# Edge-network pass of a four-layer graph kernel: target rows held as two float32r halves in place of three bf16 parts

## The chip, the cores and the metric

The kernel runs on one core of one Trainium2 chip. The metric is device time in microseconds (us) of one execution; lower is better. The median of three runs of the kernel before is 6998.53 us.

## The reference

A graph of 6250 nodes (128 features each) and 106250 edges, sorted by target, passes through four layers, each added to x after a layer norm and a relu: layer 0 (messages of neighbours and relations), layer 1 (mixture of experts, three rounds of gathering), layer 2 (the edge network), layer 3 (three dense rounds). The change is about layer 2 and the table that is made for it at the end of layer 1:

```python
def _L2_gnn_ref(x, src, dst, W1, b1, W2, b2, W4, b4):
    theta = x[dst] - x[src]
    w = sigmoid(relu(theta @ W1 + b1) @ W2 + b2)
    agg = segment_sum(w * theta, dst)
    indeg = segment_sum(ones, dst)
    return agg + indeg * (x @ W4 + b4)
```

Since (x[dst] - x[src]) @ W1 + b1 = (x @ W1 + b1)[dst] - (x @ W1)[src], the kernel makes y = x @ W1 once for each node. For each edge it then needs the row of the target, y + b1, and the row of the source, y and x.

## The kernel before

**Tiling.** Edges go in tiles of 128 (P). Four tiles (GROUP) are a group, 16 tiles (RING) a turn; there are 832 tiles, 208 groups and 52 turns. The targets of a group lie in a window of 64 nodes (WIN), since edges are sorted by target.

**Tables.** `parts_yb` holds y + b1 for each node as three bf16 parts (PARTS = 3, 384 bf16 values), whose sum is the float32 value. `rows_yh` holds y and h in float32. Both are written in the last round of layer 1 by `Layer1Out`: `late_dve` (line 1758) makes the row y + b1 in `u` and cuts it with `cut_dve` (lines 898 to 903: cut, remainder, cut, remainder), and `late_sp` (line 1724) stores `cut` and `yh`. There are 49 blocks of nodes.

**The pass** (`edge_pass` with `edge_net`, lines 442 to 790). The engines work side by side and are ordered by semaphores alone; each engine runs its own list in order.

- GpSimd (line 563) gathers the source rows of a tile, 128 rows of 1 KB, by an indirect DMA into one of 16 slots of `ring`. It waits until `tiles_done` says that the tile 16 back is finished.
- ScalarE (lines 569 to 615) issues the load of `ywin`, the 64 target rows of a group, two groups ahead (`load_window`, line 584), and of `relb`, the targets' places (line 576). It copies the finished sums of a group out of PSUM (`copy_sums`, line 591) and takes the sigmoid (line 603).
- VectorE makes the one-hot matrices: `onehot_t`, 64 x 1024 for 8 tiles (line 637), and `onehot` (line 639). `dots` (lines 646 to 654) makes the hidden layer and its product with W2 for a group; line 664 weights the one-hot by the sigmoid (`onehot_w`); lines 693 and 695 add the sums of a group to `acc`.
- TensorE brings the target rows to the edges (`hidden_net`, line 715): for each tile, three products `onehot_t` x part into `zt`, 64 x 128 weights and 128 columns (line 725). Line 756 sums the weighted source rows by target (`by_target`, one float32 product for each tile, 129 columns). `turn_sums` (lines 735 and 736) turns the sums of a group.

**Order on TensorE for a group n** (`net_tile`, line 739): the products of `zt` for tiles 0, 1 and 2 of group n+1, `turn_sums(n-1)`, `zt` for tile 3 of group n+1, then a wait for `onehot_w` of group n and the four products of `by_target`, which raise `tiles_done`. Between them lie the products of `Layer2` for a block of nodes (lines 1852 to 1862), spread over 16 tiles or so by `over` (line 488). The load of `ywin` is awaited before tile 0 of a group.

Of the kernel before, what the change touches and what calls it, by code (L numbers as in the profile page):

```python
# [7 lines left out]
D = 128  # L8
H = 256
# [3 lines left out]
P = 128  # L13

GROUP = 4
WIN = 64
RING = 16
HALF = RING // 2
GROUPS = RING // GROUP
# [14 lines left out]
NPAD = NB * P  # L34
# [28 lines left out]
FP = mybir.dt.float32  # L63
F16 = mybir.dt.float16
B16 = mybir.dt.bfloat16
PARTS = 3
LAST_GROUP = TURNS * GROUPS - 1
YH = 2 * D
FR = mybir.dt.float32r
I32 = mybir.dt.int32  # L70
U32 = mybir.dt.uint32
ALU = mybir.AluOpType
# [82 lines left out]
def gnn_kernel(nc, t, out):  # L155
    ctx = ExitStack()
    with ctx:
# [3 lines left out]
        def dram(name, shape, dt=FP):  # L161
            return nc.dram_tensor(name, shape, dt, kind="Internal").ap()
# [8 lines left out]
        def sbuf(name, shape, dt=FP):  # L171

            uses[0] += 1
            return nc.sbuf_tensor(f"{name}_{uses[0]}", shape, dt)
# [8 lines left out]
        rows256 = [dram(f"rows256_{k}", [NPAD, H]) for k in range(2)]  # L183

        parts128 = [dram(f"parts128_{k}", [NPAD, PARTS * D], B16) for k in range(2)]
        parts256 = [dram(f"parts256_{k}", [NPAD, PARTS * H], B16) for k in range(2)]
        rows_yh = dram("rows_yh", [NPAD, YH])
        parts_yb = dram("parts_yb", [NPAD, PARTS * D], B16)
        x_first = dram("x_first", [NPAD, D])
        x_rows = dram("x_rows", [NPAD, D])  # L190
        rdeg_dram = dram("rdeg_dram", [NPAD])
# [250 lines left out]
        def edge_pass(table, width, work, edge_net=None, prologue=None):  # L442
# [11 lines left out]
            with ExitStack() as tmp:  # L454
# [10 lines left out]
                    names += ["fold_pe", "fold_act", "fold_dve", "fold_own"]  # L465
                if edge_net:
                    (w2, b2) = edge_net
                    onehot_t = tmp.enter_context(sbuf("onehot_t", [WIN, 2, HALF * P], B16))
                    relb = tmp.enter_context(sbuf("relb", [WIN, 2, HALF * P]))
                    ywin = tmp.enter_context(sbuf("ywin", [WIN, GROUPS, PARTS * D], B16))  # L470
                    hidden = tmp.enter_context(sbuf("hidden", [P, GROUP, D]))
                    dot = tmp.enter_context(sbuf("dot", [P, 2, GROUP]))
                    weight = tmp.enter_context(sbuf("weight", [P, 2, GROUP]))
                    onehot_w = tmp.enter_context(sbuf("onehot_w", [P, 2, GROUP, WIN]))
                    zt = tmp.enter_context(psum("zt", [P, 2, GROUP, P]))
                    by_target = tmp.enter_context(psum("by_target", [WIN, 2, 512]))
                    held_sums = tmp.enter_context(sbuf("held_sums", [WIN, 2, D + 1]))
                    names += ["rel_loaded0", "rel_loaded1", "z_done", "net_own", "dot_done", "weight_done",
                              "weighted", "copied", "turned"] + [f"ywin_loaded{g}" for g in range(GROUPS)]

                def programs(block, sems, loop):

                    sem = dict(zip(names, sems))
# [85 lines left out]
                    def _(act):  # L569
# [10 lines left out]
                        def load_window(i, g):  # L580
                            w = act.value_load(win[0:1, bass.ds(i * GROUPS + g, 1)], min_val=0, max_val=SPARE)

                            act.wait_ge(tiles_done, i * RING + GROUP * (g + 1))
                            act.dma_start(ywin[:, g, :], parts_yb[bass.ds(w, WIN), :]).then_inc(sem[f"ywin_loaded{g}"], 16)

                        def copy_sums(n):

# [122 lines left out]
                    def _(pe):  # L710
# [4 lines left out]
                        def hidden_net(i, k):  # L715

                            g, q = divmod(k, GROUP)
                            if k % HALF == 0:
                                pe.wait_ge(onehot_ready, i * 2 + (k // HALF + 1))

                            pe.wait_ge(gathered[k], i * 16 + 16)
                            if q == 0:
                                pe.wait_ge(sem[f"ywin_loaded{g}"], i * 16 + 16)
                            for c in range(PARTS):
                                last = nc.tensor.matmul(zt[:, g % 2, q, :], onehot_t[:, g // 2, (k % HALF) * P:(k % HALF + 1) * P],  # L725
                                                        ywin[:, g, c * D:(c + 1) * D], start=(c == 0), stop=(c == PARTS - 1))
                            if q == GROUP - 1:
                                last.then_inc(sem["z_done"], 1)

# [197 lines left out]
        def rows_of(table, b, lo=0, hi=None):  # L927
            return table[bass.ds(b * P, P), lo:(hi or table.shape[1])]
# [91 lines left out]
        class Layer1(Work):  # L1020
# [12 lines left out]
            ACT_LATE = ""  # L1033
            DVE_LATE = "mix6 next_row" + Work.CUT

# [508 lines left out]
        class Layer1Out(Layer1):  # L1544
# [7 lines left out]
            DVE = Layer1.ROUTE + "mix0 mix1 mix2 mix3 down_b0 down_b1 down_b2 down_b3 mix4 mix5 with_row"  # L1552
            PE_LATE = "down2 down3 h2_t h2_w"
            ACT_LATE = "norm_root h_row h2_t_sb"
            DVE_LATE = "mix6 mix7 new_x " + Work.NORM_DVE + " next_y y_b1" + Work.CUT + " next_h"

            def __init__(self, cur, w, last):
                super().__init__(cur, None, w)
# [2 lines left out]
            def buffers(self, tmp):  # L1561
                s, p = super().buffers(tmp)
                s |= {n: tmp.enter_context(sbuf(n, sh)) for n, sh in
                      (("rt", [P, 2, P]), ("x", [P, D]), ("st", [P, 12]), ("hn", [P, D]), ("hnt", [P, P]), ("u", [P, D]),
                       ("part", [P, D]), ("yh", [P, YH]))}
                return s, p

            def fold_banks(self, n):
# [155 lines left out]
            def late_sp(self, sp, m, i, b):  # L1724
                s, _ = self.b
                sp.wait_ge(self.sem["block_out"], i * 48 + 16)
                sp.nop(nofuse=True)
                sp.dma_start(s["x"][:, :], rows_of(x_rows, b)).then_inc(self.sem["late_in"], 16)
                yield 4
                m.need(self.dve2, "new_x")  # L1730
                self.stored(m, [(rows_of(x_rows, b), s["x"][:, :])])
                m.need(self.dve2, "next_h")
                self.stored(m, [(rows_of(parts_yb, b), s["cut"][:, 0:PARTS * D]), (rows_of(rows_yh, b), s["yh"][:, :])])
                if not self.in_pass:
                    sp.wait_ge(self.sem["block_out"], i * 48 + 64)
                    sp.nop(nofuse=True)
                yield RING
# [20 lines left out]
            def late_dve(self, dve, m, i, b):  # L1758
                s, p = self.b
# [21 lines left out]
                dve.wait_ge(self.sem["block_out"], i * 48 + 16)  # L1781
                m.done("next_y", nc.vector.tensor_copy(s["yh"][:, 0:D], p["misc"][:, 0:D]))
                m.done("y_b1", nc.vector.tensor_tensor(s["u"][:, :], p["misc"][:, 0:D], self.last["b1"], ALU.add), wait=True)
                self.cut_dve(m, s["u"][:, :], s["left"][:, 0:D], [s["cut"][:, c * D:(c + 1) * D] for c in range(PARTS)])
                m.done("next_h", nc.vector.tensor_copy(s["yh"][:, D:H], s["hn"][:, :]))

        class Layer2(Work):
# [76 lines left out]
        def edge_codes(block_base, column_of, places, begin, wn, wl, embp):  # L1864
# [10 lines left out]
            with ExitStack() as tmp:  # L1875
# [19 lines left out]
                with phase(nc, bank, "own_s", "consts", "shifted", "masked", "compared", "counted", "coded", "spilled",  # L1895
# [87 lines left out]
                    def _(sp):  # L1983
# [4 lines left out]
                        sp.wait_ge(zeroed, 1)  # L1988
                        sp.dma_start(emb[0:RELS - whole, REL_BLOCKS - 1, :], t["L0_gnn_rel_emb"][whole:RELS, :]).then_inc(loaded, 16)
                        spare = []  # L1990
                        for table, width in ((rows256[0], H), (rows256[1], H), (rows_yh, YH)):
                            spare += [table[SPARE:NPAD, c:c + P] for c in range(0, width, P)]
                        for dst in spare:
                            sp.dma_start(dst, zeros[:, :]).then_inc(stored, 16)
                        spare16 = []
                        for table, width in ((parts256[0], PARTS * H), (parts256[1], PARTS * H), (parts_yb, PARTS * D)):
                            spare16 += [table[SPARE:NPAD, c:c + P] for c in range(0, width, P)]
                        for dst in spare16:
                            sp.dma_start(dst, zeros[:, 0:P // 2].bitcast(B16)).then_inc(stored, 16)
# [1252 lines left out]
        with ExitStack() as lay:  # L3252
            w = expert_tables(lay)
# [49 lines left out]
```

## Time and profile before

| | us |
|---|---|
| median of three runs | 6998.53 (6994.68 to 7003.74) |
| profiled execution, from its first to its last instruction | 7889.6 |
| of it, the passes of layer 1 that gather (2250 to 5190) | 2940 |
| of it, the edge-network pass (5190 to 6520) | 1330 |
| of it, the dense rounds of layer 3 (6600 to 7890) | 1290 |

The profiled execution is the only one with a trace. It is 891 us longer than the median of the runs, and the trace does not say which stages that time belongs to. PE is TensorE, PEld its weight loads, DVE VectorE, ACT ScalarE, POOL GpSimd, SP SyncE. The granted clock is given as a share of 2.4 GHz: 0.50 is the lower level, 1.2 GHz. Busy times of PE are unions of pipelined instructions, each of which is longer than the distance to the next one. A float32 product shows as two weight loads and two matmuls, a bf16 product as one of each.

### The profile page before, as it was taken

To read this page: it belongs to the slowest core of one execution; us is meant where nothing else is said; L and a number is where in the kernel's file an instruction comes from. 1 tells how busy PE (TensorE), PEld (TensorE's weight loads), DVE (VectorE), ACT (ScalarE), POOL (GpSimd) and SP (SyncE) were. 2 spreads that over 40 slices of the span, in tenths; PEclk is the share of its full clock that TensorE was granted. 3 is DMA by queue.
4 is the path that set the end of the run, shared out by engine and by line. 5 is a ranking of instruction groups with operands and counts; after the bars stand their busy time and mean duration, and the time that the engine had idled before them with its cause. 6 is when DMAs were issued, how large, how long until landed. Compare 5 with 4: busy or idle time off the path is not lost. (4 is left out here: it accounts for less than half of the span.)

```text
span 7889.6 us, 137900 instructions
## 1 busy us (share of the span) xinstructions
PE 6633.2 (84%) x47136; PEld 4683.6 (59%) x47136; DVE 3780.3 (48%) x11316; ACT 2080.9 (26%) x6122; POOL 2537.4 (32%) x2577
## 2 busy tenths in 40 slices
PE   4999789999978888887777877867777777999999
PEld 2555446666657777776666666645555554555555
DVE  7787534444444444443444444456666662222111
ACT  3555312222222222222333333322222220000000
POOL 0000000000035555554555555546666660000000
PEclk6999989999989999998999998955555558999999
DMA  5343442222245445444455454434444446555654
GB/s 160 107 136 113 131 131 88 89 88 86 78 124 148 144 143 145 141 141 138 138 144 145 142 144 138 138 89 126 127 125 126 126 124 201 196 193 196 200 192 160
DMA packets 669788, 1085.73 MB, mean 138 GB/s; under 512 B 247170, under 2 KB 495206, under 8 KB 667043
## 3 DMA queue, kind: packets, MB, share of 16 engines
q1 hardware_dynamic: 474722, 508.53, 21.1%
q0 software_dynamic: 147584, 438.73, 19.7%
q10 hardware_dynamic: 46784, 129.65, 4.6%
q8 instruction: 379, 6.21, 0.3%
q14 instruction: 319, 2.61, 0.1%
HBM read 902.64 MB, written 174.06 MB: 136 GB/s over the span
## 5 line engine op out<-in xcount | busy, mean ns | idle before, releaser
L563 POOL DMA_INDIRECT ring<-parts,src_idx x1664 | 1626.4, 977 | 1314.1 <-issue 444.7
L2695 PE MATMUL agg_ps<-sheet,big 128*128 128x448 f16 x6090 | 1182.0, 354 | 23.6 <-DMA sheet<-adj 23.6
L563 POOL DMA_INDIRECT ring<-rows_yh,src_idx x832 | 840.0, 1010 | 540.7 <-issue 226.0
L1099 ACT ACTIVATE strong<-hid,s_b 128x128 f32<-128x128 f32 x2352 | 668.3, 369 | 1160.9 <-PE hid L1208 441.1
L2695 PEld LDWEIGHTS agg_ps<-sheet,big 128*128 128x128 bf16 x6090 | 598.2, 99 | 565.8 <-DMA sheet<-adj 25.9
L1208 PE MATMUL hid<-agg,big 128*128 128x128 f32 x6272 | 806.3, 281 | 62.2 <-issue 51.6
L1208 PEld LDWEIGHTS hid<-agg,big 128*128 128x128 f32 x6272 | 774.9, 197 | 136.0 <-issue 119.1
L1196 PE MATMUL y<-big,strong 128*128 128x256 f32 x3136 | 742.8, 385 | 13.7 <-issue 12.0
L683 DVE TENSOR_TENSOR acc<-acc,sums 128x128 f32 x416 | 120.3, 289 | 1120.8 <-DMA acc<-in_edge_type 759.5
L1196 PEld LDWEIGHTS y<-big,strong 128*128 128x128 f32 x3136 | 586.4, 191 | 98.4 <-issue 18.5
L713 PE MATMUL sums<-onehot,ring 128*128 128x64 bf16 x9984 | 412.0, 196 | 174.8 <-issue 134.8
L1233 PE MATMUL hid<-big,agg 128*128 128x512 f32 x784 | 513.1, 788 | 35.7 <-DVE agg L1115 33.4
L713 PEld LDWEIGHTS sums<-onehot,ring 128*128 128x128 bf16 x9984 | 378.5, 100 | 272.7 <-issue 254.6
L756 PE MATMUL by_target<-ring,onehot_w 128*64 128x129 f32 x1664 | 408.8, 427 | 139.0 <-DVE onehot_w L664 109.0
L1110 DVE SCALAR_TENSOR_TENSOR row<-y,gate,row 128x256 f32<-128x256 f32 x392 | 191.1, 487 | 531.7 <-PE y L1196 433.5
L756 PEld LDWEIGHTS by_target<-ring,onehot_w 128*64 128x64 f32 x1664 | 328.4, 223 | 184.5 <-issue 184.5
L2359 PE MATMUL counts_ps<-hot_col,hot 128*128 128x392 bf16 (+3 forms) x1960 | 349.8, 300 | 90.4 <-DVE hot_col L2226 86.4
L3032 POOL MEMSET acc<- 128x6400 f32 x1 | 5.4, 5432 | 1164.5 <-PE counted_ps L3066 1164.5
L725 PE MATMUL zt<-ywin,onehot_t 64*128 64x128 bf16 x2496 | 344.4, 306 | 16.2 <-DMA ring<-rows_yh,src_idx 12.8
L1087 ACT ACTIVATE weak<-weak 128x512 f32<-128x512 f32 x294 | 184.8, 628 | 643.7 <-DVE weak L1139 571.3
L2914 DVE SCALAR_TENSOR_TENSOR agg<-agg_ps,counts_hold,acc 128x448 f32<-128x448 f32 x42 | 28.7, 684 | 674.3 <-PE agg_ps L2695 674.3
L2226 DVE TENSOR_SCALAR hot_col<-column_of,held 128x539 bf16<-128x539 f16 (+2 forms) x1176 | 337.4, 344 | 0.0
(443 smaller groups left out, 9757.7 us busy)
## 6 DMA issues: line engine op xcount, KB each, us to landing
sheet<-adj SPq DMA_DIRECT2D x294, 784.0 KB, 4.1
sheets<-adj SPq DMA_DIRECT2D x74, 784.0 KB, 4.2
adj<-big ACTq DMA_DIRECT2D x7, 5488.0 KB
adj<-acc ACTq DMA_DIRECT2D x7, 5488.0 KB
relb<-rel_rows ACTq DMA_DIRECT2D x106, 256.0 KB
ring<-parts,src_idx POOLq DMA_INDIRECT x1664
big<-adj SPq DMA_DIRECT2D x24, 784.0 KB, 4.7
parts<-cut SPq DMA_DIRECT2D x98, 192.0 KB, 1.9
```

The costliest lines, as they stand in the source:

```text
L563: nc.gpsimd.indirect_dma_start(ring[:, k, 0:YH] if edge_net else ring[:, k, :], None, table, bass.IndirectOffsetOnAxis(ap=src_idx[:, i * R ...
L713: return nc.tensor.matmul(ap, lhs, rhs, start=first, stop=last, skip_group_check=True)
L725: last = nc.tensor.matmul(zt[:, g % 2, q, :], onehot_t[:, g // 2, (k % HALF) * P:(k % HALF + 1) * P], ywin[:, g, c * D:(c + 1) * D], start ...
L756: last = nc.tensor.matmul(by_target[:, g % 2, 0:D + 1], onehot_w[:, g % 2, j, :], ring[:, g * GROUP + j, D:YH + 1], start=(j == 0), stop=( ...
L1099: ins = nc.scalar.activation(s["strong"][:, e % 2, j, :], p["hid"][:, bank_at, j * P:(j + 1) * P], ACT.Relu, bias=self.w["s1_b"][:, e, j:j ...
L1110: m.done(name, nc.vector.scalar_tensor_tensor(out=out, in0=expert, scalar=self.b[0]["gate"][:, e:e + 1], in1=so_far, op0=ALU.mult, op1=ALU ...
L1196: ins = nc.tensor.matmul(y, s["strong"][:, e % 2, k, :], w["s2"][:, k, e, :], start=(k == 0), stop=(k == 3))
L1208: ins = nc.tensor.matmul(p["hid"][:, bank_at, j * P:(j + 1) * P], w["s1"][:, k, e, j * P:(j + 1) * P], s["agg"][:, k, :], start=(k == 0), ...
L1233: ins = nc.tensor.matmul(hid, s["agg"][:, k, :], w["weak"][:, k, 2 * q:2 * q + 2, :].rearrange("p e f -> p (e f)"), start=(k == 0), stop=( ...
L2226: last = nc.vector.tensor_scalar(hot_col[:, w % 2, cut_at[j]:cut_at[j + 1]], column_of[:, lo * NODE_BLOCKS:hi * NODE_BLOCKS], held[:, r, n ...
L2359: return nc.tensor.matmul(ap, lhs, rhs, start=first, stop=last, skip_group_check=True)
L2695: ins = nc.tensor.matmul(ps[:, 0:HALF_COLS], rows_in[:, k * per + s, c, :], sheet[:, k, s * HALF_COLS:(s + 1) * HALF_COLS], start=(k == fi ...
```

## The change

The table `parts_yb` becomes `halves_yb`, two float32 values for each feature; the first is the value written as float32r, the second what is left. In the edge pass `ywin` and `onehot_t` are float32r, and each tile takes two products where it took three. `Layer1Out` makes the halves with one copy and one subtraction instead of four operations.

```diff
-        parts_yb = dram("parts_yb", [NPAD, PARTS * D], B16)
+        halves_yb = dram("halves_yb", [NPAD, 2 * D])
...
-                    onehot_t = tmp.enter_context(sbuf("onehot_t", [WIN, 2, HALF * P], B16))
+                    onehot_t = tmp.enter_context(sbuf("onehot_t", [WIN, 2, HALF * P], FR))
-                    ywin = tmp.enter_context(sbuf("ywin", [WIN, GROUPS, PARTS * D], B16))
+                    ywin = tmp.enter_context(sbuf("ywin", [WIN, GROUPS, 2 * D], FR))
...
-                            act.dma_start(ywin[:, g, :], parts_yb[bass.ds(w, WIN), :]).then_inc(sem[f"ywin_loaded{g}"], 16)
+                            act.dma_start(ywin[:, g, :].bitcast(FP), halves_yb[bass.ds(w, WIN), :]).then_inc(sem[f"ywin_loaded{g}"], 16)
...
-                            for c in range(PARTS):
+                            for c in range(2):
                                 last = nc.tensor.matmul(zt[:, g % 2, q, :], onehot_t[:, g // 2, (k % HALF) * P:(k % HALF + 1) * P],
-                                                        ywin[:, g, c * D:(c + 1) * D], start=(c == 0), stop=(c == PARTS - 1))
+                                                        ywin[:, g, c * D:(c + 1) * D], start=(c == 0), stop=(c == 1))
...
+                s["y2"] = tmp.enter_context(sbuf("y2", [P, 2 * D], FR))
...
-                self.stored(m, [(rows_of(parts_yb, b), s["cut"][:, 0:PARTS * D]), (rows_of(rows_yh, b), s["yh"][:, :])])
+                self.stored(m, [(rows_of(halves_yb, b), s["y2"][:, :].bitcast(FP)), (rows_of(rows_yh, b), s["yh"][:, :])])
...
-                self.cut_dve(m, s["u"][:, :], s["left"][:, 0:D], [s["cut"][:, c * D:(c + 1) * D] for c in range(PARTS)])
+                m.done("high", nc.vector.tensor_copy(s["y2"][:, 0:D], s["u"][:, :]), wait=True)
+                m.done("low", nc.vector.tensor_tensor(s["y2"][:, D:2 * D], s["u"][:, :], s["y2"][:, 0:D].bitcast(FP),
+                                                      ALU.subtract))
```

The zeroing of the spare rows at the start takes two float32 stores for the new table where it took three bf16 stores.

## Rows read from the trace of the kernel before

**Rows 1.** Three stages by windows: busy time, instructions, granted clock, DMA share.
```profile
core 0: us, PE busy (x) PEld busy (x) DVE busy (x) ACT busy (x) POOL busy (x), PEclk, DMA share, GB/s
2250.00:5190.00 2940.00, 2382.15 (x22109) 1968.55 (x22109) 1340.98 (x4367) 847.77 (x2460) 1626.35 (x1664) 0.90 0.49 142
5190.00:6520.00 1330.00, 930.59 (x5072) 676.94 (x5072) 866.44 (x2177) 314.55 (x800) 840.01 (x832) 0.50 0.44 125
6600.00:7890.00 1290.00, 1266.03 (x7115) 714.38 (x7112) 242.05 (x756) 108.93 (x415) 20.97 (x36) 0.99 0.58 193
```

**Rows 2.** The gathers on POOL: durations, first and last start; two single ones.
```profile
L563 POOL DMA_INDIRECT ring<-rows_yh,src_idx x832: 940/946/1454, 5194.9 to 6499.8; - x167
...
5607.81 0.94 POOL L563 DMA_INDIRECT ring<-rows_yh,src_idx  x1 [0.30 <-issue]
5609.06 0.95 POOL L563 DMA_INDIRECT ring<-rows_yh,src_idx  x1 [0.30 <-issue]
```

**Rows 3.** Waits of 5190 to 6525: who, for whom, us in total, times, longest.
```profile
DVE hidden L646 <- DMA sheets<-adj: 288.7, 62, 7.2
POOL ring L563 <- issue: 226.0, 715, 1.9
PE sums L735 <- ACT held_sums L591: 178.5, 85, 7.0
POOL ring L563 <- DMA acc<-in_edge_type: 147.8, 62, 3.0
PE by_target L756 <- DVE onehot_w L664: 109.0, 77, 3.4
```

**Rows 4.** Timeline of TensorE in the edge pass, then one gather: start, length, instruction, count.
```profile
5604.20 1.14 PE L725 MATMUL zt<-ywin,onehot_t 64*128 64x128 bf16 x9
5605.13 0.31 PE L735 MATMUL sums<-ident,held_sums 64*128 64x64 f32 x1
5605.68 0.50 PE L725 MATMUL zt<-ywin,onehot_t 64*128 64x128 bf16 x3
5606.11 1.98 PE L756 MATMUL by_target<-ring,onehot_w 128*64 128x129 f32 x8
5608.02 0.80 PE L1862 MATMUL pa<-w,ht 128*128 128x128 f32 x2
...
5612.42 0.94 POOL L563 DMA_INDIRECT ring<-rows_yh,src_idx  x1 [2.42 <-DMA acc<-in_edge_type]
```

**Rows 5.** Lengths of single PE records by line: min/median/max in ns.
```profile
L725 PE MATMUL zt<-ywin,onehot_t x2496: 216/311/311, 5200.0 to 6511.2; 64*128 64x128 bf16 x192
...
L756 PE MATMUL by_target<-ring,onehot_w x1664: 422/422/476, 5207.8 to 6517.4; 128*64 128x129 f32 x185
...
L1857 PE MATMUL pb<-ones,wsum x98: 347/358/368, 5255.5 to 6526.6; 1*128 1x1 f32 x98
...
L2759 PE MATMUL xt_ps<-ident,acc x147: 272/273/303, 6591.5 to 7865.8; 128*128 128x128 f32 x147
```

**Rows 6.** Four-byte neighbours on PE: a run of transposes at full clock, and one-column products.
```profile
6625.67 0.60 PE L2759 MATMUL xt_ps<-ident,acc 128*128 128x128 f32 x4
...
5255.45 0.58 PE L1857 MATMUL pb<-ones,wsum 1*128 1x1 f32 x2
```

**Rows 7.** VectorE groups by form: the one-hot, and the nearest writes of four bytes.
```profile
L637 DVE TENSOR_SCALAR onehot_t<-relb,iota_col 64x1024 bf16<-64x1024 f32 x105 | 78.9, 751 | 7.9 <-DMA relb<-rel_rows 7.8
L2903 DVE TENSOR_SCALAR acc<-big 128x512 f32<-128x512 f32 x14 | 6.0, 427 | 0.5
L1925 DVE TENSOR_SCALAR int<-acc 128x1024 int32<-128x1024 int32 x2 | 2.2, 1104 | 0.0
```

**Rows 8.** The cut in the last pass of layer 1 (4050 to 5190), VectorE by form.
```profile
L901 DVE TENSOR_TENSOR left<-u,cut 128x128 f32<-128x128 f32 x40 | 11.7, 293 | 1.4
L900 DVE CAST cut<-u 128x128 bf16<-128x128 f32 x40 | 10.2, 254 | 1.4
L902 DVE CAST cut<-left 128x128 bf16<-128x128 f32 x40 | 9.1, 226 | 1.4
```

**Rows 9.** DMA of 5190 to 6520: a queue's packets, MB and share; one issue.
```profile
q10 hardware_dynamic: 25280, 38.13, 9.9%
...
ywin<-parts_yb ACTq DMA_DIRECT2D x210, 48.0 KB
```

More of the change, by code:

```diff
@@ L1554, in gnn_kernel @@
             ACT_LATE = "norm_root h_row h2_t_sb"
-            DVE_LATE = "mix6 mix7 new_x " + Work.NORM_DVE + " next_y y_b1" + Work.CUT + " next_h"
+            DVE_LATE = "mix6 mix7 new_x " + Work.NORM_DVE + " next_y y_b1 high low next_h"
             def __init__(self, cur, w, last):
@@ L1990, in _ @@
                         spare = []
-                        for table, width in ((rows256[0], H), (rows256[1], H), (rows_yh, YH)):
+                        for table, width in ((rows256[0], H), (rows256[1], H), (rows_yh, YH), (halves_yb, 2 * D)):
                             spare += [table[SPARE:NPAD, c:c + P] for c in range(0, width, P)]
@@ L1995, in _ @@
                         spare16 = []
-                        for table, width in ((parts256[0], PARTS * H), (parts256[1], PARTS * H), (parts_yb, PARTS * D)):
+                        for table, width in ((parts256[0], PARTS * H), (parts256[1], PARTS * H)):
                             spare16 += [table[SPARE:NPAD, c:c + P] for c in range(0, width, P)]
```

## The prediction

> **What bounds the kernel now.** I read the stages by windows first. The change touches one of them, the edge-network pass, 1330 of 7889.6 us, and a few operations of the pass before it [rows 1]. In the edge pass no engine is full: PE is busy 930.6 us (70%), DVE 866.4, POOL 840.0, and the clock of TensorE is at its lower level, 0.50, throughout; the layer-1 passes, where PE is busy 81%, have 0.90, the dense rounds at 98% have 0.99 [rows 1]. Then the gathers: one takes 0.946 us and 0.30 of issue before it, so 1.25 us, and 832 of them 1040 us; the first starts at 5194.9 and the last at 6499.8, 1305 us apart [rows 2]. That is 6.27 us for a group of four where POOL alone would need 5.0. The other 265 us are gathers that wait for a free slot, and slots come free when `by_target` on PE is done: the wait of 2.42 us in the timeline is one of them, and the waits list holds 62 like it, 147.8 us, named after a DMA that has nothing to do with it [rows 3, 4]. So the pass is a loop: gather, `zt` on PE, `dots` on DVE, sigmoid on ACT, `onehot_w` on DVE, `by_target` on PE, slot free, gather. PE's share of it, for one group, is 930.6 / 208 = 4.47 us; POOL's floor under it is 5.0 us.
>
> The profiled execution is 891 us longer than the median of the runs. VectorE's 288.7 us of waits before `hidden`, under the name of a DMA that doesn't belong there, come while PE's own records run on without a gap [rows 3, 4]; if such waits are smaller in the runs, the pass there is nearer to POOL's floor: scaled by 6998.5 / 7889.6 it would be 1180 us. I work out differences on the profiled execution and carry them over in us, and say where the floor would cut them.
>
> **The change part by part.** *The products of `zt`.* Before: nine matmuls in 1.14 us, the last 0.31 long, so (1.14 - 0.31) / 8 = 0.104 us each at clock 0.50, and three of them 0.312 us for a tile [rows 4, 5]. After: two float32r products. The trace has none. Bounds: as cheap as bf16, 0.104; or as dear as a float32 product, which is two records: eight records of `by_target` in 1.98 us are (1.98 - 0.42) / 7 = 0.22 each, 0.44 for a product [rows 4, 5]. Between them lies what I take for nearest: an operation that shows as a single record with operands of four bytes and 128 columns. That is the float32 transpose, four in 0.60 us at the full clock: (0.60 - 0.27) / 3 = 0.11, which is 0.22 at clock 0.50 [rows 1, 5, 6]. A second row points the same way: two records with 128 columns of float32 weights and one column of data take 0.58 us, so the second comes 0.58 - 0.36 = 0.22 us after the first although there is nothing to stream, and it is the load of four-byte weights that paces them [rows 5, 6]. I take 0.21 for a float32r product, two for a tile: 0.42, which is 0.11 us more than the three bf16 products. Over 832 tiles: +92 us of PE time. With the ends: 2 x 0.104 - 0.312 = -0.104, -87 us; and 2 x 0.44 - 0.312 = +0.57, +473 us.
>
> How much of +92 reaches the end: tiles 0 to 2 of a group stand before `turn_sums`, and that waits for ACT's copy in 85 of 208 groups [rows 3]; there their +0.33 us is hidden. In the other 123 groups it shows, 41 us. Tile 3 stands right ahead of `by_target`: 208 x 0.11 = 23 us. Where `by_target` waits for `onehot_w` anyway, in 77 groups [rows 3], it is hidden too: (41 + 23) x 131 / 208 = 40 us. POOL gives nothing back, since its waits for slots end with `by_target`; but in a run near its floor part of it would be covered. I take +40, between 0 and +92.
>
> *VectorE's one-hot.* `onehot_t` takes 0.751 us for 1024 columns and will write four bytes instead of two [rows 7]. A scalar compare with four bytes in and out takes 0.427 us for 512 columns, so it can stay at 0.75 to 0.8; the dearest row of that kind and size is 1.104 us, +0.35 x 105 = +37 us of DVE time, on an engine busy 65% [rows 1, 7]. A faster one is excluded by no row, but the present rate is already half the dearest. I take nothing, up to +15 of the 37 on the loop.
>
> *The load of `ywin`.* 64 rows of 1024 bytes, not 768. It is issued two groups ahead, some 12 us; its queue is 9.9% busy [rows 9]. It would cost only if it landed after tile 0 is due. Nothing. No instruction is added on ACT, and nothing queues behind it.
>
> *Layer1Out.* Two operations fewer for each of 49 blocks (0.226 and 0.293 us and some 0.035 each): 49 x 0.59 = 29 us of DVE time in a pass where DVE is busy 46% [rows 1, 8]. They are late work, awaited by SP's store alone, whose rows grow from 768 to 1024 bytes. Between 0 and -5 us; I take 0. The zeroing at the start is one small store less, 0.
>
> **The rivals.** *One pass at the bf16 rate (faster).* If a float32r product costs 0.104 us, PE loses 87 us of work. By the same shares (0.31 us in 123 groups, 0.104 in 208, times 131 / 208) 38 us reach the loop, 87 at most. For it: a float32 record of `by_target` takes 0.22 us for 129 columns, some 264 cycles of 1.2 GHz, two a column, as if the parts of a value went in one after the other; a type that sends one part would take one [rows 4, 5]. Against it: the single-record transpose and the paced weight loads [rows 6]. Time 6998.5 - 38 = 6960. The Trainium skill, "FP8 and Floating Point Precision", TensorE Precision Notes, says that the array works natively at about 22 bits, that a reduced-precision float32 operand is read as four bytes and truncated to that, and that true float32 takes four passes; by it this rival would hold. Against the change speaks "TensorE: Matmul & The Clock Gate", Weight-path perf modes: the fast weight load is for types other than float32. The trace has no float32r row to settle it.
>
> *Four passes, or the rate of float32 at this width (slower, much).* Each product 0.44 us: PE's work grows from 930.6 to 1404 us and PE becomes the bound of the pass. For it: every float32 product of the trace pays twice two cycles a column, at 129 columns as at 128 [rows 4]. Against it: it needs two records for each product, and the transposes show that four-byte operands can go in one [rows 6]. The pass would take 1404 us if PE has no gap: 1404 - 1330 = +74 in the profile, +224 against a pass of 1180, and +473 if all is added. I take +300: 7300. It decides as soon as PE needs more than POOL's 5.0 us for a group, that is from 4.47 + 0.53 us a group, or 0.22 us for a float32r product, on.
>
> *The clock rises (faster).* The pass has 0.50 at a PE share of 70%, its neighbour 0.90 at 81% [rows 1]. If the new products make PE denser (+92 or +473 us), the full clock might be granted. Every PE record would go at about twice the rate, 2.4 GHz for 1.2, the loop would shorten, and the 265 us of POOL's waits would largely go: some -150, 6850. Against it: a share of (930.6 + 92) / 1370 = 75% is nearer to the old value, and the gaps between the groups stay.
>
> **How the numbers follow.** Chances: the forecast (a product of 0.13 to 0.25 us) 0.39; one pass at the bf16 rate 0.25; float32's rate 0.26; the clock rises 0.10. The predicted time is the forecast's: 6998.5 + 40 = 7039, and its own range is 6990 to 7105 (0 to +92, and the +15 of VectorE). The range over all cases goes from 6950 (most of the bf16 case) to 7420 (most of the float32 case). Some 0.2% (14 us) is what a measurement of this kernel can tell from no change. Faster by more: 0.17 of the bf16 case's 0.25 and 0.09 of the clock's 0.10, 0.26. Within: 0.07 + 0.10 of the forecast + 0.01 = 0.18. Slower: 0.29 + 0.26 + 0.01 = 0.56.
>
> **What would show it.** In the profile after, the group of L725 has 1664 records if a float32r product is one record, 3328 if it is two. Six matmuls of `zt` in a row (tiles 0 to 2) give the price of one by their length: 0.83 us at 0.104, 1.4 at 0.21, over 2.4 at float32's rate. PE's busy time in the pass would be some 845, 1020 or 1400 us. The granted clock of the pass should stay 0.50, POOL's first and last gather should be about 1345 us apart, and L637 should stay under 0.8 us. The prediction is wrong if the clock of the pass rises, if `zt` is at bf16's rate and POOL's waits shrink with it, or if another stage (layer 1, layer 3) moves by more than 10 us.

## The result, and the profile after

The changed kernel takes 7028.43 us (median of 5 runs, 7024.16 to 7036.13); the kernel before, on the same chip, 6995.59 us (5 runs, 6994.68 to 7003.74). The ratio is 1.0047 with a 95% interval of 1.0035 to 1.0058: 33 us slower. I had forecast 40 us slower, for the right price of a product but, as the runs show, with a wrong picture of what bounds the pass.

The profiled execution of after has a span of 7034.4 us; it is the longest of the five, 8 us over their median. Its edge pass by windows (start:end and length, then busy us and instructions of PE, PEld, DVE, ACT and POOL, granted clock, DMA share, GB/s), with the stages around it:

```profile
0.00:2250.00 2250.00, 2020.33 (x12640) 1301.95 (x12640) 1309.38 (x3962) 802.77 (x2417) 40.85 (x40) 0.95 0.35 107
2263.00:4537.00 2274.00, 2119.66 (x22109) 1838.47 (x22109) 1311.10 (x4271) 850.87 (x2460) 1631.18 (x1664) 0.97 0.64 184
4544.00:5664.00 1120.00, 1038.90 (x4237) 826.61 (x4237) 864.69 (x2170) 317.81 (x800) 835.62 (x829) 0.50 0.55 150
5744.00:7034.00 1290.00, 1266.97 (x7119) 715.27 (x7119) 241.83 (x756) 108.95 (x415) 21.02 (x36) 0.99 0.60 194
```

[rows 1] answers to these, but it can't be subtracted from them: its edge pass has 1330 us, and its layer-1 passes 2940. The first experiment is therefore a fresh profile of the kernel before. The products themselves can be read at once, in the timeline of the same sequence as [rows 4]:

```profile
5000.14 1.54 PE L725 MATMUL zt<-ywin,onehot_t 64*128 64x128 f32 x6
5001.48 0.33 PE L735 MATMUL sums<-ident,held_sums 64*128 64x64 f32 x1
...
5002.04 0.68 PE L725 MATMUL zt<-ywin,onehot_t 64*128 64x128 f32 x2
5002.65 1.98 PE L756 MATMUL by_target<-ring,onehot_w 128*64 128x129 f32 x8
```

Six float32r products in 1.54 us, where nine bf16 ones took 1.14; the fourth tile's two in 0.68, where three took 0.50. So one costs (1.54 - 0.41) / 5 = 0.226 us, and a group of four tiles 0.40 + 0.18 = 0.58 us more, 121 us over 208 groups. The groups of the pass, by line (count, min/median/max ns, first and last start; then two with busy us, mean ns | idle before):

```profile
L725 PE MATMUL zt<-ywin,onehot_t x1664: 412/412/473, 4544.4 to 5656.5; 64*128 64x128 f32 x185
L563 POOL DMA_INDIRECT ring<-rows_yh,src_idx x832: 942/949/1815, 4540.4 to 5645.7; - x167
...
L637 DVE TENSOR_SCALAR onehot_t<-relb,iota_col 64x1024 fp32r<-64x1024 f32 x105 | 79.2, 754 | 7.5 <-DMA relb<-rel_rows 7.5
L563 POOL DMA_INDIRECT ring<-rows_yh,src_idx x832 | 838.5, 1008 | 331.7 <-issue 244.4 <-PEq L781 63.9 <-PE by_target L756 23.4
```

1664 records: one for each product. The one-hot takes 754 ns, 751 before [rows 7]: four bytes out cost the same as two.

### The profile page after: what moved, and what is told of

Its sections match the earlier page's. It is cut to its first block and busy times, and to the rows that moved or that the text cites. A ratio compares the mean times of both kernels' runs of the same rounds, so it can differ in the third digit from the quotient of the medians.

```text
span 7034.4 us, 136086 instructions
## 1 busy us (share of the span) xinstructions
PE 6485.9 (92%) x46304; PEld 4705.8 (67%) x46304; DVE 3749.8 (53%) x11218; ACT 2088.8 (30%) x6122; POOL 2540.7 (36%) x2577
## 5 line engine op out<-in xcount | busy, mean ns | idle before, releaser
L563 POOL DMA_INDIRECT ring<-rows_yh,src_idx x832 | 838.5, 1008 | 331.7 <-issue 244.4
L1208 PEld LDWEIGHTS hid<-agg,big 128*128 128x128 f32 x6272 | 741.5, 192 | 41.0 <-issue 36.0
L1208 PE MATMUL hid<-agg,big 128*128 128x128 f32 x6272 | 758.5, 276 | 0.0
L725 PE MATMUL zt<-ywin,onehot_t 64*128 64x128 f32 x1664 | 473.2, 429 | 24.4 <-DMA ring<-rows_yh,src_idx 20.4
L725 PEld LDWEIGHTS zt<-ywin,onehot_t 64*128 64x128 f32 x1664 | 387.9, 318 | 139.8 <-issue 102.4
L713 PEld LDWEIGHTS sums<-onehot,ring 128*128 128x128 bf16 x9984 | 358.3, 99 | 164.3 <-issue 82.4
L713 PE MATMUL sums<-onehot,ring 128*128 128x64 bf16 x9984 | 382.5, 194 | 87.7 <-DMA ring<-parts,src_idx 85.4
L756 PE MATMUL by_target<-ring,onehot_w 128*64 128x129 f32 x1664 | 410.6, 428 | 50.2 <-DVE onehot_w L664 50.1
L1233 PE MATMUL hid<-big,agg 128*128 128x512 f32 x784 | 391.6, 623 | 0.0
```

The source lines that it names most:

```text
L563: nc.gpsimd.indirect_dma_start(ring[:, k, 0:YH] if edge_net else ring[:, k, :], None, table, bass.IndirectOffsetOnAxis(ap=src_idx[:, i * R ...
L713: return nc.tensor.matmul(ap, lhs, rhs, start=first, stop=last, skip_group_check=True)
L756: last = nc.tensor.matmul(by_target[:, g % 2, 0:D + 1], onehot_w[:, g % 2, j, :], ring[:, g * GROUP + j, D:YH + 1], start=(j == 0), stop=( ...
L1208: ins = nc.tensor.matmul(p["hid"][:, bank_at, j * P:(j + 1) * P], w["s1"][:, k, e, j * P:(j + 1) * P], s["agg"][:, k, :], start=(k == 0), ...
L1233: ins = nc.tensor.matmul(hid, s["agg"][:, k, :], w["weak"][:, k, 2 * q:2 * q + 2, :].rearrange("p e f -> p (e f)"), start=(k == 0), stop=( ...
```

## The experiments

**The kernel before, profiled again.** No edit.

> The kernel before, unchanged, for a second profile: the profiled execution on record was 7889.6 us long against a median of 6995.6 us. If those 891 us belong to that one execution (theory: waits of other engines for TensorE's signals, which came late), the new profile is within 50 us of 6996, the edge-network pass is 1060 to 1110 us and not 1330, and VectorE's waits before hidden under a DMA's name are gone. If they belong to the kernel whenever it is profiled (rival), it is again near 7890 and the pass near 1330.

Measured: 6992.95 us, with a span of 6991.2. The excess of 891 us in the profile that I predicted from was that one execution's. The windows of this execution, layer-1 passes, edge pass and layer 3:

```profile
2250.00:4525.00 2275.00, 2115.76 (x22109) 1837.93 (x22109) 1339.72 (x4371) 849.51 (x2460) 1625.82 (x1664) 0.97 0.64 183
4532.00:5621.00 1089.00, 926.79 (x5069) 668.98 (x5069) 863.36 (x2170) 317.06 (x800) 821.70 (x829) 0.50 0.56 151
5701.00:6991.00 1290.00, 1266.49 (x7119) 713.96 (x7119) 241.90 (x756) 108.93 (x415) 20.98 (x36) 0.99 0.60 193
```

The edge pass takes 1089 us, not 1330, with the same busy times as [rows 1] to within 2.3%, POOL's 840 against 822 the furthest off. Its gathers:

```profile
L563 POOL DMA_INDIRECT ring<-rows_yh,src_idx x832: 940/946/1506, 4528.1 to 5605.0; - x167
...
L563 POOL DMA_INDIRECT ring<-rows_yh,src_idx x832 | 824.7, 991 | 320.0 <-issue 236.7 <-PEq L781 66.8 <-PE by_target L756 16.5
```

Without the 66.8 us before the first one, the idle time is 253.2 us, 0.305 for each of 831 gaps, and in the timeline none of the gaps is over 0.32 us; every gather from the 17th on begins at least 3.3 us after `by_target` has freed its slot. The 16.5 us that are put down to `by_target` lie within such gaps. So the gathers run one behind the other without waiting for a slot: 832 x (0.991 + 0.305) = 1078 us of the pass's 1089. *POOL's chain of gathers is the bound of the pass before*, which [rows 2, 3] had not shown: there gathers waited some 212 us for slots. TensorE is busy 85% and does the waiting (line waited for: total us, times, longest):

```profile
PE zt L725 <- DMA ring<-rows_yh,src_idx: 71.5, 105, 2.0
PE by_target L756 <- DVE onehot_w L664: 49.6, 43, 1.9
PE sums L735 <- ACT held_sums L591: 32.2, 39, 1.7
PE zt L725 <- DVE onehot L639: 11.0, 1, 11.0
```

Against these stand the waits of after in its own edge pass:

```profile
PE by_target L756 <- DVE onehot_w L664: 50.1, 47, 1.7
PE zt L725 <- DMA ring<-rows_yh,src_idx: 20.4, 22, 10.3
PE sums L735 <- ACT held_sums L591: 14.8, 29, 1.1
```

Now the sum closes. PE is busy 1038.9 - 926.8 = 112 us more. Its idle time in the pass falls from 1089 - 926.8 = 162 to 1120 - 1038.9 = 81 us. Net +31, the pass's 1089 to 1120, and nearly all of the kernel's +33. The waits say what gave way: `zt` waited 82.5 us (71.5, and 11.0 once at the start of the pass) and now 20.4, of which 10.3 is that same start; `turn_sums` 32.2 and now 14.8. The wait for `onehot_w` gave nothing: 49.6 and 50.1. The gathers now span 1105.3 us from first to last instead of 1076.9: their instructions last 13.8 us longer in sum (838.5 against 824.7), and the gaps 14.6 (267.8 against 253.2), ten of them over 0.5 us, where a gather really waited for a slot. So POOL's chain grew by two parts of about the same size, and the next experiments must account for both.

Outside the pass these two profiled executions also differ: after's layer-1 passes begin 13 us later. Its first gather of layer 1 is at 985.1 us, that of before at 974.4; but in cut_back below, which has the same change, it is at 975.8. Those 11 us are of that one execution, and not of the change.

**Less and more work for TensorE, with the type left alone.** If the gathers are the floor, taking products away gains next to nothing, and adding them costs less than their length. In the kernel before, the third product of each tile is left out (the third part of `y_b1` is missing from the sum), or made twice (it counts double):

```
-                            for c in range(PARTS):
+                            for c in range(2):              (bf16_two)
+                            for c in (0, 1, 2, 2):          (bf16_four)
...
```

> The kernel before with the third bf16 product left out (y + b1 lacks its smallest part), TensorE has 87 us less. Theory (the gathers on GpSimd are the floor): 0 to 15 us under the kernel before. Rival (the pass follows TensorE in proportion, as my prediction's working had it): 30 to 87 us under it.

> The kernel before with a fourth bf16 product for each tile (the third part's product a second time, so y + b1 has its smallest part twice). Theory: what the float32r products cost is TensorE's time in the loop; the fourth product adds 0.104 us a tile, 87 us of TensorE, against some 0.14 us a tile (115 us) in the changed kernel, so this kernel is 15 to 35 us over the one before. Rival: the cost lies in what comes with four-byte data (longer load of ywin, write of onehot_t, weight loads that hold up others), and 87 us more of bf16 on TensorE cost 0 to 8 us.

**One float32r product instead of two.** In the kernel after, the low half is left out. Everything else of the change is there: the four-byte one-hot, the wider rows, the wider load.

```
-                            for c in range(2):
+                            for c in range(1):
...
-                                                        ywin[:, g, c * D:(c + 1) * D], start=(c == 0), stop=(c == 1))
+                                                        ywin[:, g, c * D:(c + 1) * D], start=True, stop=True)
```

> The changed kernel with the first float32r product alone (the low half is left out of y + b1); tables, loads and one-hot stay float32r. TensorE has 0.225 us for a tile, less than three bf16 products. Theory (TensorE's time is the cost): back at the kernel before or up to 15 us under it. Rival (four-byte data cost it): still 15 to 35 us over the kernel before.

Measured: bf16_two 6981.78 us against 6987.96, ratio 0.9991 (0.9982 to 1.0000); fr_one 6988.72, 0.9999 (0.9990 to 1.0008); bf16_four 7005.90, 1.0023 (1.0014 to 1.0032). Their edge passes by windows, in this order:

```profile
4527.00:5611.00 1084.00, 856.74 (x4237) 571.60 (x4237) 862.06 (x2170) 316.80 (x799) 820.33 (x829) 0.50 0.56 152
```
```profile
4535.00:5621.00 1086.00, 896.39 (x3405) 658.54 (x3405) 864.25 (x2170) 316.72 (x800) 819.14 (x829) 0.50 0.58 155
```
```profile
4528.00:5634.00 1106.00, 1004.12 (x5901) 762.62 (x5901) 863.85 (x2169) 317.11 (x798) 838.33 (x829) 0.50 0.55 149
```

In one table, by PE's busy time in the pass (after with its difference from the first section):

| kernel | PE busy, us | against before | share of the pass | pass, us | mean gather, us | kernel against before, us |
|---|---|---|---|---|---|---|
| bf16_two | 856.7 | -70 | 79% | 1084 | 0.990 | -6 |
| fr_one | 896.4 | -30 | 83% | 1086 | 0.989 | +1 |
| before | 926.8 | 0 | 85% | 1089 | 0.991 | 0 |
| bf16_four | 1004.1 | +77 | 91% | 1106 | 1.011 | +18 |
| after | 1038.9 | +112 | 93% | 1120 | 1.008 | +33 |

The time follows PE's work, but not in proportion. 70 us less of it bring 6 us (the interval allows 0 to 13): the waits for gathered rows take it up.

```profile
PE zt L725 <- DMA ring<-rows_yh,src_idx: 157.3, 214, 2.7
```

That is bf16_two, 157.3 us where before has 71.5. 77 us more cost 18, about a quarter; the last 35, from bf16_four to after, cost 15, nearly a half. And fr_one, with all of the float32r data but one product, is at the time of before (the interval allows 7 us less to 6 us more): the type, the one-hot, the rows and the load cost nothing that shows. bf16_four is slower without any float32r. So what costs is the time that more products take on TensorE.

How that time reaches the end isn't the same in the two slower kernels. In bf16_four no gap between gathers is over 0.5 us, so no gather waits for a slot. Its gathers span 1093.5 us, 17 more than before, and all of that is their mean length, 832 x (1.011 - 0.991) = 17 us. It isn't the four-byte one-hot (bf16_four writes bf16, and fr_one, which writes four bytes, has 0.989). The timeline of bf16_four, POOL beside VectorE, shows what it goes with:

```profile
4847.54 0.95 POOL L563 DMA_INDIRECT ring<-rows_yh,src_idx  x1 [0.30 <-issue]
4848.01 0.69 DVE L646 TENSOR_TENSOR hidden<-zt,ring 128x512 f32<-128x512 f32 x1 [1.79 <-PE zt L725]
4848.74 0.69 DVE L649 SCALAR_TENSOR_TENSOR hidden<-hidden,w 128x512 f32<-128x512 f32 x1
4848.80 1.45 POOL L563 DMA_INDIRECT ring<-rows_yh,src_idx  x1 [0.31 <-issue]
4849.46 0.69 DVE L654 TENSOR_REDUCE dot<-hidden 128x4 f32<-128x512 f32 x1
```

Beside the first gather `hidden` starts after 0.47 us, and the gather takes its usual 0.95. Beside the second the reduce into `dot` starts after 0.66 us, and the gather takes 1.45: it ends at 4850.25, 0.10 us after the reduce. This holds for every gather of the traces: one beside which that reduce starts 0.25 to 0.70 us after its own start ends 0.09 to 0.11 us after the reduce's end. Gathers beside the one-hot `onehot_t` have a mean of 1.11 us in the kernel before. Beside `hidden` (lines 646 and 649), just as long, they keep their 0.95. The time above 0.946 us a gather, in sum:

| kernel | gathers with such a reduce | their excess, us | of others beside `onehot_t`, us | of the rest, us |
|---|---|---|---|---|
| bf16_two | 30 | 8.0 | 22.0 | 6.2 |
| fr_one | 24 | 7.6 | 21.3 | 6.6 |
| before | 27 | 7.4 | 22.8 | 7.5 |
| bf16_four | 76 | 25.0 | 23.2 | 5.9 |
| after | 67 | 20.9 | 22.8 | 7.7 |

The first kind alone grows: +17.6 us in bf16_four, +13.5 in after, which is all of the gathers' longer time. So more work on TensorE shifts VectorE's reduce against the beat of the gathers, and more gathers meet it. Only in after does the other part come in, the 14.6 us of gaps, since slots now come free late. No run moves the reduce alone: that it holds the gather up is read from the ends in the traces, and how many gathers meet it isn't a function of TensorE's busy time that these runs would show.

**The removed cut operations put back.** In after, two more VectorE operations for each block of Layer1Out, on a tile that nobody reads:

```
+                m.done("again0", nc.vector.tensor_copy(s["cut"][:, 0:D], s["u"][:, :]), wait=True)
+                m.done("again1", nc.vector.tensor_tensor(s["cut"][:, D:2 * D], s["u"][:, :], s["cut"][:, 0:D],
+                                                         ALU.subtract))
```

> The changed kernel with two operations more for each block at the end of layer 1 (a cast and a subtraction of 128 x 128 into a buffer that is not read), as many as the change removed. Theory: the removed operations were off the path, so within 5 us of the changed kernel. Rival: they gave back up to 29 us that the edge pass then lost, and this kernel is 10 to 29 us over the changed one.

Measured: 7018.61 us against 6989.31, ratio 1.0044 (1.0030 to 1.0058), where after has 1.0047. The two operations are off the path. The windows agree: VectorE has 1311.1 us in the layer-1 passes of after and 1339.7 in before, the 29 us of the sum, and the passes are 2274 and 2275 us long. The edge pass of cut_back, 4527 to 5647, has the 1120 us of after.

**The price of a float32r product by its sizes.** Ahead of layer 3 stands a stretch of TensorE work of its own, sixteen products of each size in a row, at the clock of 0.50 that the edge pass left:

```
+                        runs = [(FR, WIN, P, 128), (FR, WIN, P, 64), (FR, P, P, 128), (FR, WIN, 32, 128), (B16, WIN, P, 128), (FR, WIN, P, 256), (FR, WIN, P, 512), (B16, WIN, P, 512)]
...
+                                    nc.tensor.matmul(ps[0:cols, n, 0:wide], wt[0:rows, 0:cols], mt[0:rows, 0:wide], start=True, stop=True)
```

> The changed kernel with a stretch of TensorE work added before layer 3, three times runs of 16 products each: float32r with 64 rows of weights and 128 weight columns at 128, 64, 256 and 512 columns of data, with 128 rows, with 32 weight columns, and bf16 at 128 and 512. If the weight load paces a float32r product (theory), 64 and 128 columns cost the same 0.22 us at clock 0.50, 32 weight columns at 128 columns of data cost about 0.11, and 512 columns 0.43. If the data paces it at two cycles a column (rival), 64 columns cost 0.11, 32 weight columns change nothing, and 512 columns cost 0.85.

Measured, in rows by form, each from a stretch with one size alone (rows * columns of the weights, then rows x columns of the data; min/median/max ns, first and last start):

```profile
L3296 PE MATMUL micro_ps<-mf,wf x16: 412/412/472, 5659.4 to 5662.6; 64*128 64x128 f32 x16
...
L3296 PE MATMUL micro_ps<-mf,wf x15: 398/398/398, 5663.0 to 5666.0; 64*128 64x64 f32 x15
...
L3296 PE MATMUL micro_ps<-mf,wf x15: 415/415/415, 5666.6 to 5669.6; 128*128 128x128 f32 x15
...
L3296 PE MATMUL micro_ps<-mf,wf x16: 305/305/313, 5669.9 to 5671.5; 64*32 64x128 f32 x16
...
L3296 PE MATMUL micro_ps<-mb,wb x16: 311/311/327, 5671.6 to 5673.3; 64*128 64x128 bf16 x16
...
L3296 PE MATMUL micro_ps<-mf,wf x16: 412/412/559, 5673.3 to 5676.7; 64*128 64x256 f32 x16
...
L3296 PE MATMUL micro_ps<-mf,wf x16: 625/625/625, 5676.9 to 5683.3; 64*128 64x512 f32 x16
...
L3296 PE MATMUL micro_ps<-mb,wb x15: 631/631/647, 5683.7 to 5689.7; 64*128 64x512 bf16 x15
```

The length of a record is not its price: records overlap. The price is the distance of the starts, last less first, over the count less one:

| weights, data | float32r | bf16 |
|---|---|---|
| 128 columns, 64 of data | 3.0 / 14 = 0.21 | |
| 128 columns, 128 of data | 3.2 / 15 = 0.21 | 1.7 / 15 = 0.11 |
| 128 rows and columns, 128 of data | 3.0 / 14 = 0.21 | |
| 128 columns, 256 of data | 3.4 / 15 = 0.23, and 0.21 from the second on | |
| 128 columns, 512 of data | 6.4 / 15 = 0.43 | 6.0 / 14 = 0.43 |
| 32 columns, 128 of data | 1.6 / 15 = 0.11 | |

With 64, 128 or 256 columns of data the price is the same, 0.21 us, so the data doesn't set it; with 32 columns of weights instead of 128 it halves, to what 128 columns of data take by themselves. With 512 columns of data float32r costs what bf16 does, 0.43 us, one column a cycle of 1.2 GHz. So the data of float32r goes at the rate of bf16, and it is the load of 128 four-byte weight columns that takes 0.21 us, two cycles of 1.2 GHz a column, and shows as soon as it lasts longer than the data. The kernel's products have 128 and 128: there the load sets the price, and float32r is twice as dear as bf16. The Trainium skill, "TensorE: Matmul & The Clock Gate", Weight-path perf modes, says that the fast weight load has no win for float32; these rows agree, for float32r: 0.21 against at most 0.11 us. The Trainium skill, "FP8 and Floating Point Precision", TensorE Precision Notes, says that true float32 takes four passes, and gives no rate for the reduced precision. The trace agrees on float32: two records of 0.22 us for 129 columns [rows 4], two cycles a column each. The rate of a single pass, which I concluded for a rival, holds here for the data alone.

**Both halves in one product.** The contraction uses 64 of the array's 128 rows. The halves can be stacked, high on partitions 0 to 63 and low on 64 to 127, with the one-hot made for both, so that one product with 128 rows does the work of two. TensorE then has fewer products than before; what it costs is a `relb` broadcast to twice the partitions, and two loads for `ywin`, each issued by ACT. The same for bf16: the first and the second part stacked, the third alone, two products for three.

```
-                    onehot_t = tmp.enter_context(sbuf("onehot_t", [WIN, 2, HALF * P], FR))
-                    relb = tmp.enter_context(sbuf("relb", [WIN, 2, HALF * P]))
-                    ywin = tmp.enter_context(sbuf("ywin", [WIN, GROUPS, 2 * D], FR))
+                    onehot_t = tmp.enter_context(sbuf("onehot_t", [2 * WIN, 2, HALF * P], FR))
+                    relb = tmp.enter_context(sbuf("relb", [2 * WIN, 2, HALF * P]))
+                    ywin = tmp.enter_context(sbuf("ywin", [2 * WIN, GROUPS, D], FR))
...
+                            for c in range(2):
+                                act.dma_start(ywin[c * WIN:(c + 1) * WIN, g, :].bitcast(FP), halves_yb[bass.ds(w, WIN), c * D:(c + 1) * D]).then_inc(sem[f"ywin_loaded{g}"], 16)
```

> The changed kernel with both halves in one product: the one-hot stands twice (128 partitions), the high half of the window's rows in partitions 0 to 63 and the low half in 64 to 127. It computes all that the changed kernel does, with one float32r product of 128 rows for each tile: 0.225 us of TensorE where the kernel before has 0.312 (-72 us). One more load of ywin for each group, and relb goes to 128 partitions, twice the bytes. Theory (TensorE's time, with the gathers as floor): like the float32r kernel with one product, 0 to 10 us under to 5 over the kernel before. Rival (the doubled loads collide with the gathers): 10 to 40 us over it.

> The kernel before with parts one and two in one product of 128 rows and the third in a second: two bf16 products, 0.208 us a tile, and nothing left out; doubled relb load and one more ywin load, as in the stacked float32r kernel. Theory: like the kernel with two bf16 products, 3 to 10 us under the kernel before. Rival (the loads collide with the gathers): 0 to 30 us over it.

Measured: fr_stacked 7003.86 us against 6989.31, ratio 1.0020 (1.0011 to 1.0029); bf16_stacked 7006.77, 1.0024 (1.0014 to 1.0034). Both slower than before, where I had expected them level or faster, and both faster than after. In fr_stacked PE is busy only 859.5 us of the 1060 from 4540 to 5600, so it isn't TensorE's work. Over that stretch the queue that ACT issues to, and the two waits of PE and ACT that grew:

```profile
q10 hardware_dynamic: 46944, 66.26, 19.2%
...
ACT held_sums L593 <- issue: 106.4, 48, 3.0
...
PE sums L737 <- ACT held_sums L593: 75.9, 45, 3.4
```

In the same stretch of the kernel before:

```profile
q10 hardware_dynamic: 24480, 36.79, 12.3%
...
ACT held_sums L591 <- issue: 76.5, 47, 3.0
...
PE sums L735 <- ACT held_sums L591: 30.5, 38, 1.4
```

PE waits 45 us longer for ACT's copy, and the idle time of ACT before that copy in which it waits for nothing shown ("issue") is 30 us more: between two copies ACT now issues two loads and not one. bf16_stacked shows the same, 62.0 us of waits for the copy. So both grew with the doubled loads. Whether the copy comes late through ACT's issuing or through the bytes isn't separated, since both grew in both kernels. Nor did the pass grow by PE's waits as they stand; what it grew by is seen on POOL. In fr_stacked the gathers span 7 us more than before, 6.5 of them longer gathers (44 meet the reduce, not 27), and only two gaps are over 0.5 us. In bf16_stacked they span 10 us more: the gaps are 16 us longer in sum, with sixteen over 0.5 us, and the gathers 6 us shorter.

**One wait for a group of gathers, not for each.** If the 0.305 us between gathers are the wait and the no-op that POOL executes before each, leaving three of four out lowers the floor. In the kernels before, after, and both stacked ones:

```
+                                if not edge_net or k % GROUP == 0:
-                                pool.wait_ge(tiles_done, i * RING + (k + 1))
-                                pool.nop(nofuse=True)
+                                    pool.wait_ge(tiles_done, i * RING + (k + 1))
+                                    pool.nop(nofuse=True)
```

> The kernel before, with GpSimd in the edge pass waiting for tiles_done once for each group and not before each of its four gathers (tiles_done rises by four at a time, so the other three waits never hold). Theory: the gathers at 1.296 us each are the floor of the pass before the change; without wait and no-op in three of four, the 0.305 us between gathers falls to 0.05 to 0.2 there, the pass gets 60 to 130 us shorter until TensorE (927 us busy of 1089) or the slots hold it, and the kernel is 30 to 100 us faster. Rival (the loop through TensorE and VectorE sets the pace, the gathers merely follow): within 8 us of the kernel before.

> The changed kernel with the same edit on GpSimd. Theory: TensorE is its bound already (1039 us busy of 1120), so it gains little, 0 to 25 us, and stands 60 to 112 us behind the kernel before with that edit: with the gathers' floor lowered the 112 us that the change puts on TensorE show in full. Rival (both are held by the gathers, whose instructions merely last longer after the change): it gains as much as the kernel before does, and the distance stays at 33 us.

> The stacked float32r kernel (one product of 128 rows for each tile) with the edit on GpSimd. TensorE has 30 to 70 us less than in the kernel before. If TensorE is the bound once the gathers are quicker, it is 10 to 60 us faster than the kernel before with that edit; if its doubled loads of relb and ywin cost what they seem to cost (some 15 us), it is level with it or behind.

> The stacked bf16 kernel (two products for each tile) with the edit on GpSimd. Some 75 us less on TensorE than the kernel before. Same theory and rival as for the stacked float32r kernel: 10 to 60 us faster than the kernel before with that edit, or level with it.

Measured, against 6987.81 us: lean_before 6991.54, ratio 1.0002 (0.9993 to 1.0011); lean_after 7017.76, 1.0043 (1.0029 to 1.0057); lean_fr_stacked 7001.46, 1.0021 (1.0012 to 1.0030); lean_bf16_stacked 7009.97, 1.0031 (1.0019 to 1.0043). The gap didn't shrink, as POOL's row of lean_before shows beside that of before:

```profile
L564 POOL DMA_INDIRECT ring<-rows_yh,src_idx x832 | 826.5, 993 | 315.7 <-issue 238.0 <-PEq L782 62.5 <-PE by_target L757 15.2
```

(315.7 - 62.5) / 831 = 0.305 us, the same; the 30 to 100 us that I had expected of lean_before didn't come, and the other three stand where they stood without the edit. So the edit did nothing to the floor, and what a lower floor would bring stays open; the 0.305 us belong to the gathers themselves, however few waits stand between. No kernel that computes all of the reference's work came out faster than the one before.

## Why the prediction was right, and where not

**The price of the product** (step: 0.21 us, two for a tile, +0.11 us a tile, +92 us). Right in kind: the neighbour that decided was the load of four-byte weights, which took 0.22 us with one column of data [rows 5, 6], and the widths show that this is the mechanism. Slightly short in size: in the kernel a product costs 0.226 us, since the first of each row takes 0.27 us and not 0.21, and PE's busy time in the pass rose by 112 us and not 92. I forecast 1020 us, it is 1038.9. The rival of one pass at bf16's rate was right for the data and wrong for the weights; at 64 x 128 by 128 it is the weights that count. The rival of float32's rate fell with the 1664 records.

**What bounds the pass.** This is the step that failed. I read a loop in which gathers wait for slots, 265 us of them, and TensorE's time goes through to the end unless another wait covers it. Even in that profile only some 212 us were waits; the other 53 were gathers longer than the median that I multiplied by, since their sum is 840.0 us [rows 1] and not 832 x 0.946 = 787. In an execution at the usual time no gather of the kernel before waits: the pass stands on POOL's floor. I had put the floor at 5.0 us a group, 1040 us, and worked out that at 1180 us the pass would be nearer to it. The pass takes 1089, and the floor is 1078, because the mean gather is 0.991 us and not the 0.946 of the median. The waits of 2.42 us that I took for typical [rows 4] belong to that one profiled execution. With this, POOL's distance of first to last gather, forecast as 1345 us, is 1105.

**How much reaches the end** (+40 of 92). Measured: 31 of 112, or 33 for the kernel. The share is 28% where I had 43%, the sums nearly equal, because the larger price and the smaller share cancel. But the groups that I counted are not what hid it. I took off the groups in which `by_target` waits for `onehot_w`; this wait gave nothing back, 49.6 and 50.1 us. The wait of `turn_sums` for ACT's copy gave 17 us. The largest cover, 62 us, was `zt`'s wait for gathered rows, which [rows 3] doesn't list at all, as in that execution the rows were there long before. And of what did reach the end, nearly half (13.5 us) is gathers held beside VectorE's reduce, a term that my sum doesn't have. That the forecast is so near is therefore largely luck. The experiment with four bf16 products bears this out: 77 us of added work, without float32r and without a gather that waits for a slot, and 18 us at the end.

**The steps at no cost.** VectorE's one-hot (754 against 751 ns), the load of `ywin`, the cut in Layer1Out and the zeroing: all right, though the row of 0.427 us that I took for a compare [rows 7] is a maximum with zero. fr_one, which has all of them, runs at the time of before, 0.9999, and cut_back at that of after.

**The clock.** It stayed at 0.50 through the pass, though TensorE is busy 93% of it; the rival that it rises fell.

## What to carry to other kernels

A float32r product with 128 columns of weights costs the load of its weights, twice a bf16 product, unless the data behind it is wide enough to cover the load (512 columns cost the same in both types); two products for three are a loss at 128 columns (0.45 against 0.31 us a tile here) and by the same rows would be a gain at 512 (an estimate: two of 0.43 us against three). Before pricing an engine's extra work, find what bounds the stage in an execution whose time is that of the median: a profile 13% longer than the runs can show waits in a place where the runs have none. And look for the engine's own waits: added work fills them first, and only what is left moves the end (6 us for 70, 18 for 77, 33 for 112 here). What is left needn't come by the path that you priced: read the bounding engine's instructions for longer ones too, and what runs beside them.

## What the runs showed of the hardware

- A float32r product is one record of TensorE, float32's is two. Its data goes at one column a cycle as bf16's (512 columns in 0.43 us at 1.2 GHz in either type), and the load of its weights takes two cycles a column (128 columns in 0.21 us). How many rows are used, 64 or 128, makes no difference: 0.21 and 0.21.
- Between two gathers of 128 rows POOL has 0.305 us that neither waits nor no-ops account for, with one wait for each gather or for each four. With the mean of 0.991 us for the gather itself that is 1.296 us for each, and the floor of the pass.
- A gather's instruction is held up beside some operations of VectorE: it ends 0.10 us after a `dot` reduce (128 x 512 float32) that starts 0.25 to 0.70 us into it, and has 1.11 us in the mean beside `onehot_t` in the kernel before, while beside `hidden`, two operands of the same size, it keeps 0.95. That is worth 30 us of the pass before (7.4 + 22.8) and 44 of after.
- The granted clock is 0.50 from the first to the last tile of the pass with TensorE busy 79% or 93%, while its neighbours have 0.97 and 0.99 at busy shares of 93% (2119.66 of 2274 us) and 98%.
